# One transformer block in float32: a memset moved, a split moved, a copy taken out, and transposed rows copied by tile

## The reference, cut to what matters

```python
x = x + cross_attention(layernorm(x), ctx)      # 16 heads of 32, ctx is 8 x 512 tokens, softmax
x = x + linear_attention(layernorm(x))          # below
x = x + experts(layernorm(x))                   # below

# linear attention
q, k, v = split(x @ w_qkv)                      # 16 heads of 32
q_proj = elu1(q @ proj[h]); k_proj = elu1(k @ proj[h])   # 128 features a head
kv = k_proj.T @ v; z = 1 / (q_proj @ sum(k_proj) + 1e-8)
out = (q_proj @ kv * z) @ w_out + b_out

# experts: 16 routed ones and a shared one
scores = softmax(x @ gate_w.T).transpose()      # per sequence: 16 experts x 64 tokens
topk_w, topk_idx = top_k(scores, 8)             # each expert takes its 8 best tokens
h = gelu(x_tok @ Wg[e].T) * (x_tok @ Wu[e].T)
out[tok] += (h @ Wd[e].T) * topk_w              # and the same form with Ws_g, Ws_u, Ws_d for all tokens
```

## Time and profile before

| | us |
|---|---|
| median of 3 runs | 675.45 (672.86 to 676.87) |
| the profiled execution | 672.65 |
| its span | 669.5 |
| TensorE busy | 638.5 (95%) |
| VectorE busy | 319.3 (48%) |
| ScalarE busy | 254.6 (38%) |
| GpSimd busy | 36.6 (5%) |
| HBM read | 125.90 MB |

### The profile page before, as it was taken

One profiled execution on the slowest core, in us unless ns is written; L12 is line 12 of the kernel. 1 busy time (PEld: TensorE's weight loads), 2 busy tenths in 40 slices (PEclk: granted clock), 3 DMA queues, 4 the chain that ended last, 5 costly groups with the idle time before them and its releaser, 6 DMA issues.

```text
span 669.5 us, 10402 instructions
## 1 busy us (share of the span) xinstructions
PE 638.5 (95%) x4216; PEld 414.6 (62%) x4216; DVE 319.3 (48%) x646; ACT 254.6 (38%) x486; POOL 36.6 (5%) x38
## 2 busy tenths in 40 slices
PE   6989999999999999898999998999999999999997
PEld 5767777787878776576888565444444434443433
DVE  5964635445362626847778775323233232323123
ACT  5744635454454426437685252111121212211110
POOL 0300000000000002436000000000000000000000
PEclk9999999999999999999999998999999999999999
DMA  8111010110430000030319633989999999999972
GB/s 312 81 64 64 1 65 14 51 62 3 173 143 1 1 2 1 1 111 0 130 57 430 265 130 126 389 334 417 381 415 416 406 399 404 391 380 387 370 291 74
DMA packets 14347, 129.55 MB, mean 193 GB/s; under 512 B 2720, under 2 KB 2848, under 8 KB 6240
## 3 DMA queue, kind: packets, MB, share of 16 engines
q1 hardware_dynamic: 12576, 127.15, 48.7%
q10 hardware_dynamic: 1728, 1.77, 0.8%
HBM read 125.90 MB, written 1.05 MB: 190 GB/s over the span
## 4 chain that ended last, share of the span: by engine, by line
PE 78%; DVE 9%; DMA 5%; ACT 4%; issue 2%; ACTq 2%; SPq 1%; DVEq 0%
PE ps L1211 22%; PE ps L1495 14%; PE ps L1532 7%; PE ps L1505 5%; PE ps L1405 5%; DMA w_u<-in_wu 4%; PE ps L1281 4%; PE ps L1354 3%; PE ps L1545 3%; PE ps L1257 3%; PE ps L1292 2%; PE ps L1322 2%; PE ps L1444 2%; ACTq L396 2%; PE ps L1456 1%
## 5 line engine op out<-in xcount | busy, mean ns | idle before, releaser
L1495 PE MATMUL ps<-w_u,x_slot 128*64 128x512 f32 x256 | 58.1, 595 | 1.3 <-DMA w_u<-in_wu 1.3
L1532 PE MATMUL ps<-w_d,hid_T 128*64 128x512 f32 x256 | 58.2, 596 | 1.1 <-ACT hid_T L763 1.1
L1495 PE MATMUL ps<-w_g,x_slot 128*64 128x512 f32 x256 | 58.1, 595 | 0.8 <-ACT x_slot L779 0.8
L582 ACT ACTIVATE probs<-ps,neg_max 128x512 f32<-128x512 f32 x64 | 43.5, 688 | 39.1 <-DVE neg_max L898 39.1
L741 ACT ACTIVATE hid<-ps 128x512 f32<-128x512 f32 x24 | 14.4, 598 | 102.6 <-PE ps L1495 76.8
L1211 PE MATMUL ps<-wv_hi,ctx_hi 128*128 128x512 f32 x128 | 51.5, 403 | 0.0
L878 DVE COPY probs_T<-ps 128x512 f32<-128x512 f32 x28 | 19.4, 692 | 64.8 <-PE ps L1281 64.8
L1211 PE MATMUL ps<-wv_lo,ctx_hi 128*128 128x512 f32 x128 | 49.9, 390 | 0.0
L1211 PE MATMUL ps<-wv_hi,ctx_lo 128*128 128x512 f32 x128 | 49.8, 389 | 0.0
L898 DVE TENSOR_REDUCE neg_max<-ps 128x1 f32<-128x512 f32 x64 | 39.8, 684 | 18.4 <-PE ps L1257 18.3
L1073 DVE TENSOR_TENSOR hid<-hid,ps 128x512 f32<-128x512 f32 x24 | 16.5, 687 | 65.7 <-PE ps L1495 36.1
(11 more groups left out here) (248 smaller groups left out, 1194.2 us busy)
## 6 DMA issues: line engine op xcount, KB each, us to landing
w_u<-in_wu SPq DMA_DIRECT2D x16, 2048.0 KB, 15.5
w_d<-in_wd SPq DMA_DIRECT2D x16, 2048.0 KB, 11.9
w_g<-in_wg SPq DMA_DIRECT2D x16, 2048.0 KB, 13.0
ctx_raw<-in_ctx SPq DMA_DIRECT2D x7, 1024.0 KB, 4.7
w_qkv<-in_wqkv SPq DMA_DIRECT2D x1, 3072.0 KB, 15.1
ws_g<-in_wsg SPq DMA_DIRECT2D x1, 2048.0 KB, 7.7
ws_u<-in_wsu SPq DMA_DIRECT2D x1, 2048.0 KB, 7.6
ws_d<-in_wsd SPq DMA_DIRECT2D x1, 2048.0 KB, 21.0
```

Of the source, the lines that this page charges most:

```text
L582: act.activation(probs[:, p, :], bank(SCORE[p]), ACT.Exp, bias=neg_max[:, p:p + 1], scale=1.0, accum_out=row_sum[:, p:p + 1]).then_inc(exp ...
L1495: ins = pe.matmul(ps[64 * fh:64 * (fh + 1), dst, :], x_slot[:, e, dt, :], weights[e % 2][:, dt, BANK * fh:BANK * (fh + 1)], start=(dt == 0 ...
L1532: ins = pe.matmul(ps[64 * fh:64 * (fh + 1), 6 + side(n), :], hid_T[:, side(n), j, 64 * fh:64 * (fh + 1)], w_d[e % 2][:, KT * fh + j, :], s ...
```

## The change

It has four parts.

1. GpSimd clears v_bd and writes its ones ahead of all low parts of the weights; before, the four low parts of the value weights came first. Ahead of adding the second bias it also waits for both low halves of proj.
2. ScalarE makes proj_hi behind its third value copy, ahead of the key copies; VectorE makes proj_lo at the same place.
3. The transposes of att go tile by tile: each tile of rows has one PSUM bank (ATT_BANK), its four transposes are issued as soon as its rows are there (items "T" in LIN_ORDER for tiles 0 to 2; tile 3 behind the first residual product), and ScalarE alone copies each bank into att_T. The residual product of a tile waits for that tile's copy.
4. VectorE's searches read the scores in PSUM bank 7; the copy to SBUF is gone.

```diff
--- before.py
+++ after.py
@@ -293,7 +293,7 @@
         feat_ps, fexp_done, frelu_done, feat_done = (
             sem("feat_ps"), sem("fexp_done"), sem("frelu_done"), sem("feat_done"))
         kv_ps, kv_done, att_ps, att_done = sem("kv_ps"), [sem("kv_done_act"), sem("kv_done_dve")], sem("att_ps"), sem("att_done")
-        attT_ps, attT_act, attT_dve = sem("attT_ps"), sem("attT_act"), sem("attT_dve")
+        attT_ps, attT_done = sem("attT_ps"), sem("attT_done")
         logit_ps, lsub_done, lexp_done, score_done = (
             sem("logit_ps"), sem("lsub_done"), sem("lexp_done"), sem("score_done"))
         scoreT_ps, spread_done, pick_ps, pick_done = (
@@ -322,7 +322,7 @@
         ROW_BANK = 4
         LOGIT_T_BANK, LOGIT_BANK, GATHER_BANK = 2, 3, (2, 3, 6, 7)
         BY_DVE = (5, 7)
-        ATT_BANK = (0, 1, 2, 7)
+        ATT_BANK = (7, 2, 3, 5)
 
 
 
@@ -339,7 +339,7 @@
 
         for t in range(NT):
             LIN_ORDER += [("q", 2 + t // 2, 2 * t % 4), ("q", 2 + t // 2, 2 * t % 4 + 1), ("att", 0, t)]
-        LIN_ORDER += [("att", 1, t) for t in range(NT)]
+        LIN_ORDER += [("att", 1, 0), ("att", 1, 1), ("T", 0, 0), ("att", 1, 2), ("T", 0, 1), ("att", 1, 3), ("T", 0, 2)]
 
         QKV_BY = [("dve",)] * 4 + [("act", "dve")] * 4 + [("dve",)] * 4
 
@@ -502,7 +502,6 @@
                     pool.wait_ge(qkv_hi_done, i + 1)
                     pool.tensor_tensor(lo, raw, hi.bitcast(F32), ALU.subtract).then_inc(qkv_lo_done, 1)
 
-            weights_low(range(4))
             pool.wait_ge(v_ps, B * NS)
             pool.memset(v_bd[:], 0.0).then_inc(vbd_zero, 1)
             pool.wait_ge(vbd_zero, 1)
@@ -510,8 +509,9 @@
                 rows = slice(L * par, L * (par + 1))
                 pool.memset(v_bd[rows, :, :, par, HD:HD + 1], 1.0).then_inc(vbd_zero, 1)
             pool.wait_ge(vbd_zero, 3)
-            weights_low(range(4, 12))
+            weights_low(range(12))
             pool.wait_ge(rows_in, 32)
+            pool.wait_ge(proj_split, 2)
             add_row_bias(1, bout_rows)
             pool.wait_ge(res_ps, 2 * NT)
             pool.tensor_copy(expert_of[:], ident[0:E, 0:E].unsqueeze(2).to_broadcast([E, E, CAP])).then_inc(expert_map, 1)
@@ -672,13 +672,13 @@
             values_out(5)
             xn_high_linear(NT - 1)
             values_out(6)
-            for n in range(4):
-                heads_high(n, kl_halves, n)
-                qkv_high((8 + n,))
             act.wait_ge(proj_in, 64)
             for i in range(2):
                 act.activation(proj_hi[:, :, i, :], proj_twice[:], ACT.Identity,
                                scale=head_mask[:, i:i + 1]).then_inc(proj_hi_done, 1)
+            for n in range(4):
+                heads_high(n, kl_halves, n)
+                qkv_high((8 + n,))
             values_out(7)
             u = w = 0
             for kind, i, r in LIN_ORDER:
@@ -698,9 +698,10 @@
                     w += 1
                 elif kind == "p":
                     heads_high(i, ql_halves, i - 8)
-            for dt in (0, 2):
-                act.wait_ge(attT_ps, dt + 1)
-                act.copy(att_T[:, dt, :], bank(ATT_BANK[dt])).then_inc(attT_act, 1)
+            for t in range(NT):
+                act.wait_ge(attT_ps, t + 1)
+                act.copy(att_T[:, :, P * t:P * (t + 1)],
+                         bank(ATT_BANK[t]).rearrange("p (k c) -> p k c", k=KT)).then_inc(attT_done, 1)
 
             def shared_high_gu(i):
 
@@ -978,14 +979,14 @@
             values_out(5)
             xn_low_linear(NT - 1)
             values_out(6)
-            for n in range(4):
-                heads_low(n, kl_halves, n)
-            values_out(7)
             for i in range(2):
                 dve.wait_ge(proj_hi_done, i + 1)
                 dve.scalar_tensor_tensor(out=proj_lo[:, :, i, :], in0=proj_twice[:], scalar=head_mask[:, i:i + 1],
                                          in1=proj_hi[:, :, i, :].bitcast(F32), op0=ALU.mult,
                                          op1=ALU.subtract).then_inc(proj_split, 1)
+            for n in range(4):
+                heads_low(n, kl_halves, n)
+            values_out(7)
             u = w = a = 0
             for kind, i, r in LIN_ORDER:
                 if kind in "kq":
@@ -1012,7 +1013,7 @@
                         dve.tensor_copy(kv[:, r, HPT * i:HPT * (i + 1), :],
                                         ps[:, 4, 0:HPT * 2 * KVW].rearrange("p (h c) -> p h c", h=HPT)).then_inc(kv_done[1], 1)
                     w += 1
-                else:
+                elif kind == "att":
                     dve.wait_ge(att_ps, a + 1)
                     first = 3 + 2 * (a % 2)
                     got = [ps[L * par:L * (par + 1), first:first + 2, 0:HPT * 2 * KVW].rearrange(
@@ -1030,9 +1031,6 @@
                                                     [L, 2, HPT, HD]), ALU.mult)
                     ins.then_inc(att_done, 1)
                     a += 1
-            for dt in (1, 3):
-                dve.wait_ge(attT_ps, dt + 1)
-                dve.tensor_copy(att_T[:, dt, :], bank(ATT_BANK[dt])).then_inc(attT_dve, 1)
 
             def shared_low_gu(i):
                 g = g_stripe(i)
@@ -1104,12 +1102,12 @@
             link(dve.reciprocal(linv[:], lsum[:]))
             dve.tensor_tensor(logit[:], logit[:], over_experts(linv), ALU.mult).then_inc(score_done, 1)
             dve.wait_ge(scoreT_ps, 1)
-            link(dve.tensor_copy(score_T, ps[0:E, 7, :]))
+            scores = ps[0:E, 7, :]
             for b in range(B):
-                ins = dve.max(top_w[:, b, :], score_T[:, L * b:L * (b + 1)])
+                ins = dve.max(top_w[:, b, :], scores[:, L * b:L * (b + 1)])
             link(ins)
             for b in range(B):
-                ins = dve.max_index(top_i[:, b, :], top_w[:, b, :], score_T[:, L * b:L * (b + 1)])
+                ins = dve.max_index(top_i[:, b, :], top_w[:, b, :], scores[:, L * b:L * (b + 1)])
             link(ins)
             link(dve.tensor_copy(top_f[:], top_i[:]))
             odd = top_f[:].rearrange("e (t u) c -> e t u c", u=2)[:, :, 1, :]
@@ -1410,9 +1408,17 @@
                 if n == 5:
                     linear_transpose(NT - 1)
 
+            def att_transpose(t):
+                pe.wait_ge(att_done, NT + t + 1)
+                for dt in range(KT):
+                    ins = pe.transpose(ps[:, ATT_BANK[t], P * dt:P * (dt + 1)], att[:, t, P * dt:P * (dt + 1)], ident[:])
+                ins.then_inc(attT_ps, 1)
+
             u = w = a = 0
             for kind, i, r in LIN_ORDER:
-                if kind == "p":
+                if kind == "T":
+                    att_transpose(r)
+                elif kind == "p":
                     qkv_project(i)
                 elif kind in "kq":
                     if u == 0:
@@ -1458,15 +1464,6 @@
                                         start=True, stop=True)
                     ins.then_inc(att_ps, 1)
                     a += 1
-            pe.wait_ge(feat_done, 32)
-            for t in range(NT):
-                pe.wait_ge(att_done, NT + t + 1)
-                for dt in range(KT):
-                    ins = pe.transpose(ps[:, ATT_BANK[dt], P * t:P * (t + 1)], att[:, t, P * dt:P * (dt + 1)], ident[:])
-                    if t == NT - 1:
-                        ins.then_inc(attT_ps, 1)
-            pe.wait_ge(attT_act, 2)
-            pe.wait_ge(attT_dve, 2)
             pe.wait_ge(wout_in, 16)
 
             def moe_transpose(t):
@@ -1476,7 +1473,11 @@
                 ins.then_inc(xnT_ps, 1)
 
             for t in range(NT - 1):
+                pe.wait_ge(attT_done, t + 1)
                 residual(1, t, att_T, w_out)
+                if t == 0:
+                    att_transpose(NT - 1)
+            pe.wait_ge(attT_done, NT)
             moe_transpose(0)
             residual(1, NT - 1, att_T, w_out, lambda: moe_transpose(1))
             moe_transpose(2)
```

## The result

The changed kernel took 667.26 us in the median of four executions (665.99 to 668.04), the kernel before 674.85 beside it (four executions, three of them those shown above): ratio 0.9884, 95% interval [0.9848, 0.9919], so 5.5 to 10.3 us less. The forecast of 671.6 had the sign right and half of the size; its range ended at 668.8.

A forecast was written before the change was run, and what follows sets the result against it. TensorE was taken to bound the kernel (78% of the span), the end leaning on the weight stream. Steps -2.2 - 2.1 + 1.0 - 0.5 = -3.8 us gave 668.85, carried to the 675.45 median as 671.6; range 668.8 to 674.8.

The forecast's parts named there:

- Part 1: Second layer norm: VectorE no longer held by the memset, alternating with GpSimd's subtractions instead; -2.2 us, -2.6 to -2.0 or -1.2.
- Part 2: Key features: TensorE's 2.3 us wait for proj_lo goes, a 0.2 to 0.7 stall comes at the fourth; -2.1 us.
- Part 3: Attention rows: fourth copy delays ScalarE's casts, hence VectorE's residual for tile 0; +1.0 us, ends -1.8 to +1.2.
- Part 4: Router's scores: 0.7 us copy goes, sixteen searches from PSUM cost 0.01 each more; -0.5 us, ends -0.7 to 0.0.
- The half-speed stretch goes too: Under the gather: clock stays at 2.4 GHz behind the shortened spread-index wait, saving 1.4 us more, 670.2; chance 0.20.
- my slower rival: Third residual to router's logits: clock falls in new TensorE gaps, staying down through the gather; +2.5 us, 678.0; chance 0.07.
- The stream holds the end: Expert stage: weight stream sets the pace, last w_u lands as before; no change, 675.4 us; chance 0.17.

The follow-up runs named there:

- e8: Changed kernel with ScalarE's casts of gate and first shared weights ahead of the fourth attention-row copy: 664.59 us, ratio 0.9840 to the kernel before.
- e6: Kernel before, unchanged, profiled once more after e5: 676.47 us, span 674.4.
- e5: Kernel before, unchanged, profiled again: 675.76 us, span 673.3.
- e7: Kernel before with unread matmuls filling TensorE's waits for probs_T and proj_lo, both waits kept: 672.62 us, ratio 0.9961.
- e2: Kernel before with only GpSimd's clearing of v_bd moved ahead of all low parts of the weights: 671.46 us, ratio 0.9946.

## Why the prediction was wrong

*The steps of the sum* were right, each within 0.6 us of the profile, but three of the four were put too small: together -4.7 measured (with the clock in both profiles at one stretch) against -3.8. Part 1: -2.2 forecast, -2.77 measured; the alternation with GpSimd's subtractions that I bounded came for one tile of two only. Part 2: -2.1 and -2.00, with 0.3 of the new stall that I had put at 0.2 to 0.7 (my own times, 316.7 against 316.3, give at most 0.4). Part 3: +1.0 and +0.71, by the mechanism named (fourth copy, casts, low parts, residual), with the two gaps of about 1 us ahead of the transposes; e8 takes it away and gets 2.8 back. Part 4: -0.5 and -0.64.

*The step that failed* is in the paragraph on the sum: "It is 2.8 below the median of the runs shown, 675.45; carried to that median the forecast is 671.6." I carried a difference worked out in one execution to the median and took the 2.8 us between the two as an offset that the change leaves alone. It was not one. The profiled execution had one half-speed stretch, the median execution three. In e6 two of the three lie behind the very waits that parts 1 and 2 remove, in e5 one of three; filling these two waits gives back 0.0044 of the clock (e7), 1.7 stretches an execution. By the line through the 52 executions the kernel before loses 0.0070 x 500 = 3.5 us to the clock, the changed one 0.0025 x 500 = 1.2. So the change gives 2.3 us in clock and 4.9 in work: -7.2, beside -7.6 and -7.1 in the medians. Of the 3.4 us between this and the -3.8 forecast, 2.3 are the offset taken for fixed and 1.1 are the size of the steps (0.9 in the profiles).

The offset was not all clock either. The profiled execution was also the earliest of all thirteen profiles at the first product with w_o: 262.51 us, against 262.91 to 264.20 in the others, 263.70 and 264.18 in e5 and e6, with the same code ahead of it. Against the mean span of 672.8 its 669.5 is 3.3 less, of which 2.0 is clock by the line and about 1.2 this start (the median of the twelve others is 263.7); the time around its span, 3.15 against 2.1 in the mean of the 52, took 1.1 back. Why the start differs is open.

*The range* left out an end of its own: the parts' ends reach -7.4, that is 668.05, and I stopped it at 668.8. The measured 667.26 lies below both.

*The rival that came nearest* failed in the same place. "The half-speed stretch goes too" looked only at the stretch under the gather, and set against itself that "gaps as long, 2.3 at the projection, had none, so it is no plain function of the gap". That was one execution's luck read as a rule: the same gap of 2.27 us has a stretch behind it in e5 and in e6 and none in the first profile. Over all profiles in which a wait stands unfilled, a stretch lies behind the wait for probs_T in one of six, behind the one for proj_lo in three of six, and behind the one for spread_i, under the broadcast or the gather, in five of seven at 1.9 us and in four of five at 1.3. So the length of a gap alone does not settle the outcome, and the shortening by part 4 is not seen to keep the clock up. In the changed kernel's own profile the stretch under the gather did go (-1.21), and one appeared under the logits (+1.02), the place of my slower rival; it lasted 3.4 us and was paid back by the other. "The stream holds the end" is out: the shift of 4.5 us at the last gather product reached the end as 4.3.

*What stays open.* At full clock the four parts alone add to -2.2 - 2.2 + 0.8 - 0.4 = -4.0, together they give -4.9. The profiles allow a second count that leaves out the start: from the first product with w_o to the first product of the experts the three profiles of the kernel before take 150.0, 152.7 and 152.6 us with one, three and three stretches, so 1.3 a stretch and 148.7 without any. Counted so, the parts alone give -2.6, -1.9, +0.8 and -0.4, together -4.1, and the change -4.9 and -4.5 in its two profiles. Four executions of the change in each group, a slope that was taken from the kernel before, and clocks reported to 0.001 (0.5 us) leave room for the rest; I can't say whether it is more. Why the same wait is followed by a stretch in one execution and not in the next is open as well.

## What to carry to other kernels

Here a wait of about 2 us in TensorE cost its length and, in some executions, 3.41 us at 1.2 GHz behind it, worth about 1.3 us. So price the removal of such a wait at its length plus 1.3 us times the chance of a stretch; the two waits of e7 were worth 2.2 us of clock together. Where the profiled execution is faster than the median, don't carry the difference over as fixed: compare the clocks of the timed executions first. And when an operand comes late, put its copy behind whatever the next stage wants from the same engine, not ahead of it: e8 took 3 us from moving one copy.

## What the runs showed that I had not expected

- The stretches are all 3.41 us long, twice that in e5 and e2, and by the clock the same kernel has one to four of them. They don't begin with the first product behind a wait: at the wait for proj_lo the clock falls 0.2 us before the wait is over in e5 and 0.8 us after in e6, and in e7 it falls 2.5 us after the wait for spread_i.
- Beside the memset of GpSimd (from 268.77 in the kernel before) VectorE's wide tensor_scalar waits (5.03 us), two 128x1 operations just ahead of it, at 268.89 and 269.08, do not (0.15 and 0.16). Beside GpSimd's tensor_tensor a 128x1 product of two SBUF operands waits as well: 0.93 us instead of 0.16.
